# Preparing the first expert block inside the last attention unit, in a fused cross-attention and mixture-of-experts kernel

## What is computed

```python
x = x + tanh(g_xattn) * attention(k=ctx, v=ctx, q=layernorm(x))    # 16 heads of 16, relative bias, causal
x = x + tanh(g_ffn)   * moe(layernorm(x))

# moe, for N = 4096 rows, 8 experts (H = 256, I = 128) and one shared expert:
scores = sigmoid(x @ gate_w.T)                      # choose 2 of 4 groups, then 4 of 8 experts
cw     = 2.5 * normalised scores of the chosen experts, 0 for the others
out    = sum_e cw[:, e] * ((silu(x @ Wg[e]) * (x @ Wu[e])) @ Wd[e]) + shared(x)
```

## Time and profile before

| | us |
|---|---|
| median of 3 runs (683.05 to 684.8) | 683.97 |
| the profiled execution, its own time | 685.87 |
| its span, first to last instruction | 684.1 |
| PE busy | 593.5 (87%) |
| DVE busy | 429.0 (63%) |
| ACT busy | 293.7 (43%) |
| POOL busy | 197.0 (29%) |

### The profile page before, as it was taken

How to read it: one execution, slowest core, us unless ns; L and a number is a source line. 1 busy time by engine, 2 the same in 40 slices (tenths; PEclk the granted TensorE clock), 3 DMA queues, 4 the chain that set the end, 5 groups by cost and what they waited for, 6 DMA issues and landing times.

```text
span 684.1 us, 10534 instructions
## 1 busy us (share of the span) xinstructions
PE 593.5 (87%) x3256; PEld 462.2 (68%) x3256; DVE 429.0 (63%) x868; ACT 293.7 (43%) x553; POOL 197.0 (29%) x187
## 2 busy tenths in 40 slices
PE   3637897888888988886669999999999999999996
PEld 3526654556557656543458888788888888888886
DVE  5397759765877587712773856647476574756553
ACT  2443595447744685553513424233342422434221
POOL 4173035301640064001102233423323232332222
PEclk9877999999979999989679999999999999999999
DMA  5782527153433443632121031221202222031220
GB/s 168 174 213 74 115 54 176 25 126 67 120 85 83 99 119 76 173 124 51 33 78 47 6 104 47 93 61 49 76 30 93 61 78 77 1 108 47 93 63 31
DMA packets 43313, 58.13 MB, mean 85 GB/s; under 512 B 8368, under 2 KB 25520, under 8 KB 43248
## 3 DMA queue, kind: packets, MB, share of 16 engines
q1 hardware_dynamic: 42320, 56.16, 30.4%
q10 hardware_dynamic: 960, 1.57, 1.0%
HBM read 33.13 MB, written 6.11 MB: 57 GB/s over the span
## 4 chain that ended last, share of the span: by engine, by line
PE 42%; issue 28%; DVE 13%; POOL 9%; ACT 3%; DMA 2%; SPq 1%; ACTq 1%; DVEq 0%; POOLq 0%
PE py L1554 6%; PE pg L1539 6%; PE pu L1539 6%; POOL hl L1246 4%; PE work L1024 3%; PE oT L1009 3%; PE smax L944 3%; PE oT L1013 2%; DVE mx L675 2%; POOL d L454 2%; PE work L918 2%; PE sT L989 2%; PE sT L988 2%; DVE mx L703 2%; PE work L880 1%
## 5 line engine op out<-in xcount | busy, mean ns | idle before, releaser
L1246 POOL TENSOR_TENSOR hl<-sg,hh 128x512 fp32r<-128x512 f32 x72 | 93.1, 1294 | 244.0 <-ACT hh L1289 231.6
L575 ACT ACTIVATE ex<-sT 128x512 f32<-128x512 f32 (+1 forms) x160 | 92.5, 592 | 93.5 <-PE sT L989 72.8
L1283 ACT ACTIVATE sg<-pg 128x512 f32<-128x512 f32 x72 | 43.1, 598 | 196.1 <-PE pu L1539 196.0
L675 DVE TENSOR_REDUCE mx<-smax 128x2 f32<-128x308 f32 x187 | 81.4, 472 | 30.4 <-PE smax L944 29.3
L1554 PE MATMUL py<-wxl,hh 128*128 128x256 f32 x288 | 81.4, 283 | 4.1 <-DVE x L1433 2.9
L1554 PE MATMUL py<-wxh,hl 128*128 128x256 f32 x288 | 80.5, 280 | 0.0
L1554 PE MATMUL py<-wxh,hh 128*128 128x256 f32 x288 | 80.4, 279 | 0.0
L1421 DVE TENSOR_TENSOR sg<-cwb,sg 128x512 f32<-128x512 f32 x64 | 60.0, 937 | 11.2 <-DMA cwb<-cwt_d 8.3
L1539 PE MATMUL pg<-x2l,wxh 128*128 128x512 f32 x144 | 60.8, 422 | 4.1 <-issue 4.1
L1554 PEld LDWEIGHTS py<-wxl,hh 128*128 128x128 f32 x288 | 54.2, 188 | 10.3 <-DVE x L1433 5.2
L1416 DVE TENSOR_TENSOR sg<-pu,sg 128x512 f32<-128x512 f32 x72 | 49.1, 682 | 17.2 <-ACT sg L1283 15.5
(11 more groups left out here) (164 smaller groups left out, 1140.7 us busy)
## 6 DMA issues: line engine op xcount, KB each, us to landing
cwb<-cwt_d SPq DMA_DIRECT2D x64, 256.0 KB, 3.3
qs<-qh SPq DMA_DIRECT2D x56, 128.0 KB, 2.5
at<-rden_d SPq DMA_DIRECT2D x64, 64.0 KB, 2.2
out<-x SPq DMA_DIRECT2D x8, 512.0 KB, 4.5
ks<-km SPq DMA_DIRECT2D x16, 231.0 KB, 3.4
qs<-ql SPq DMA_DIRECT2D x28, 128.0 KB, 2.5
wx<-in_wx SPq DMA_DIRECT2D x9, 384.0 KB, 6.3
x<-in_x SPq DMA_DIRECT2D x3, 1024.0 KB, 13.6
```

The lines of the kernel that those rows point to most:

```text
L575: nc.scalar.activation(ex[:, g % 2, i % 5, q0:HALF], ST[i % 2][:, q0:HALF], ACT.Exp).then_inc(exp_s, 1)
L675: nc.vector.reduce_max(mx[:, first_tile(p) if start else m_tile(h, p), stk::NSTK], banks[q % len(banks)][:, 0:PAIR].rearrange("p (j k) -> ...
L1246: nc.gpsimd.tensor_tensor(hl[:, i % R, :], sg[:, i % R, :], hh[:, i % R, :], ALU.subtract).then_inc(hl_done, 1)
L1283: nc.scalar.activation(sg[:, i % R, :], PG[i % RG][:], ACT.Silu).then_inc(sg_s, 1)
```

## The change

Parts of the preparation of block 0 are moved into the last attention unit, and the order of the transition is written anew.

- **Memory.** The attention tiles `d0, d1, relc, rotc, relr, tp, sx, km` are allocated earlier, so that what the experts' stage writes early lies over tiles that are no longer used once unit 6's scores are made (`near_done`). `wxh` and `wxl` become halves of one tile `split`.
- **The last divisors.** For unit 7 the broadcast reciprocals and the divided result lie in `ex[:, 0, 0:2, :]` in place of `at` (`outputs`). `raw_done` is gone from PE.
- **Inside unit 7**, by step `i`, each engine calls `prepare`. DVE: step 0 statistics, router tables, split of expert 0 (both parts now by DVE); 4 `normalised(0)`; 7 and 10 `x_lo`; 11 split of expert 1; 13 `router_out`; 15 `logits_in` and split of expert 2; 19 `divide` of unit 6. PE: 7 and 10 `transposes`, 13 `router`, 15 `logits`. ACT: 7 and 10 `x_hi`, 19 `scores(0)`. POOL: `rstd_of(0)` and the clearing of `gst`.
- **Behind unit 7**, PE: `gate_up` 0 and 1, `weights_T`, `project(B-1, 0)`, `gate_up` 2, `project(B-1, 1)`, `gate_up` 3, then the items with those four left out. ACT: high parts of experts 3 to 8 with silu 0 and 1 among them. DVE: the order below.

```diff
+    def near_done(eng):
+
+        eng.wait_ge(st_ps, NI * (2 * B - 1))
...
+    def outputs(u):
+
+        return ex[:, 0, 0:2, :] if isinstance(u, int) and u == 2 * B - 1 else at
...
+        def prepare():                      # POOL
+            near_done(pool)
+            nc.gpsimd.memset(gst[:].bitcast(F32), 0.0).then_inc(gst_s, 1)
+            pool.wait_ge(c_in, 3 * 16)
+            rstd_of(0)
...
+        def prepare(i):                     # ACT
+            if i == 0:
+                near_done(act)
+            if i in (7, 10):
+                x_hi(0, 0, ((i - 7) // 3,))
+            if i == 19:
+                scores(0)
+
+        attend_scalar(act, prepare)
+        scores_done(act)
+        for e in range(NOWN, NE1):
             act.wait_ge(w_in[e], 16)
             nc.scalar.copy(wxh[:, e, :], wx[:, e, :]).then_inc(w_hi, 1)
-            if e == 4:
-                scores(0)
-        silu(0, 0)
+            if e in (4, 6):
+                silu(0, (e - 4) // 2)
...
+        def weights_split(e):               # DVE
+
+            dve.wait_ge(w_in[e], 16)
+            nc.vector.tensor_copy(wxh[:, e, :], wx[:, e, :]).then_inc(w_own, 1)
+            dve.wait_ge(w_own, e + 1)
+            nc.vector.tensor_tensor(wxl[:, e, :], wx[:, e, :], wxh[:, e, :], ALU.subtract).then_inc(w_lo, 1)
...
+            if i == 0:
+                near_done(dve)
+                dve.sem_inc(misc_free, 1)
+                norm_stats(0)
+                tables()
+                weights_split(0)
+            if i == 4:
+                normalised(0)
+            if i in (7, 10):
+                x_lo(0, 0, ((i - 7) // 3,))
+            if i == 11:
+                weights_split(1)
+            if i == 13:
+                router_out(0)
+            if i == 15:
+                logits_in(0)
+                weights_split(2)
+            if i == 19:
+                divide_first()
+
+        reciprocals_second, residual_first, divide_second, residual_second = attend_vector(dve, prepare)
+        scores_done(dve)
+        dve.sem_inc(gu_free, RG)
+        dve.sem_inc(h_done, R)
+        routing(0, 0)
+        routing(0, 1)
+        weights_lo(3)
+        reciprocals_second()
+        weights_in(0)
+        gated(0, 0)
+        weights_lo(4)
         residual_first()
+        gated(0, 1)
         norm_stats(1)
-        for e in range(NE1):
...
+        divide_second()
+        for e in range(5, NE1):
+            weights_lo(e)
+        weighted(0, 0)
+        weighted(0, 1)
+        residual_second()
         turns(dve, item)
...
+        def prepare(i):                     # PE
+            if i == 7:
+                pe.wait_ge(c_in, 3 * 16)
+                transposes(0, (0,))
+            if i == 10:
+                transposes(0, (1,))
+            if i == 13:
+                pe.wait_ge(gst_s, 2)
+                router(0, 0)
+            if i == 15:
+                logits(0)
+
+        attend_first, attend_finish = attend_tensor(pe, prepare)
+        exp_done(pe)
+        pe.sem_inc(hid_free, R)
+        pe.sem_inc(gu_ps, 1)
         gate_up(0, 0)
         gate_up(0, 1)
         weights_T(0)
+        attend_first()
+        gate_up(0, 2)
         attend_finish()
+        gate_up(0, 3)
         residual_done(pe)
         turns(pe, item)
```

More of the change, by code:

```diff
@@ L391, in sync, with gpsimd @@
         divisors(2 * B - 1, 1)
-    def gpsimd(pool):
+    def gpsimd(pool, prepare):
         nc.gpsimd.memset(va[:], 0.0).then_inc(pool_set, 1)
@@ L491, in unit @@
                 short_chunk(b + 1)
+            if h == 1 and not ahead:
+                prepare()
         rstd_of(0)
@@ L499, in gpsimd, with scalar @@
         batches(pool, unit)
-    def scalar(act):
+    def scalar(act, prepare):
         act.wait_ge(w_in, 5 * 16)
@@ L597, in unit @@
                     k_hi(b + 1, W[(NW0 + K_USE) % 2])
+                if h == 1 and not ahead:
+                    prepare(i)
                 if (h == 0 or ahead) and i == 19:
@@ L620, in scalar, with vector @@
         raw_out(2 * B - 1, 1, 3)
-    def vector(dve):
+    def vector(dve, prepare):
         dve.wait_ge(pool_set, 4)
@@ L808, in unit @@
                             residual(b - 1 + h, 1 - h, pr, NW0 + Y_USE[h] + pr)
+                if h == 1 and not ahead:
+                    prepare(i, lambda: divide(u - 1, 1 - h))
         dve.wait_ge(x_first, 16)
@@ L848, in first_half @@
                 residual(B - 1, 0, pr, NW0 + Y_USE[1] + pr)
-            reciprocals(2 * B - 1)
         def second_half():
@@ L854, in second_half, with tensor @@
                 residual(B - 1, 1, pr, NW0 + Y_USE[0] + pr)
-        return lambda: divide(2 * B - 2, 0), first_half, lambda: divide(2 * B - 1, 1), second_half
-    def tensor(pe):
+        return lambda: reciprocals(2 * B - 1), first_half, lambda: divide(2 * B - 1, 1), second_half
+    def tensor(pe, prepare):
         pe.wait_ge(w_in, 5 * 16)
@@ L1082, in tensor, with first @@
             values(B - 1, 1, NG - 1, short)
-        for pr in range(2):
-            project(B - 1, 0, pr, B - 1, Y_USE[1] + pr)
+        def first():
+            for pr in range(2):
+                project(B - 1, 0, pr, B - 1, Y_USE[1] + pr)
         def finish():
@@ L1142, in experts @@
     cw = sb("cw", [P, TB, E])
+    split = sb("split", [P, NE1, 2, XW], F32R)
+    wxh, wxl = split[:, :, 0, :], split[:, :, 1, :]
     cwb = sb("cwb", [P, RC, HALF])
@@ L1170, in experts @@
     block = ctx.enter_context(nc.Block())
-    RG = 2
+    RG, NOWN = 2, 3
     PER = 2 * NE1
@@ L1252, in item @@
                 rstd_of(n + 2)
-        rstd_of(0)
+        def prepare():
[3 more added lines that the diff above has]
+            rstd_of(0)
+        attend_gpsimd(pool, prepare)
+        scores_done(pool)
+        pool.sem_inc(hl_done, R)
         rstd_of(1)
@@ L1292, in item @@
             n, e, ahead = place(k, i, last)
-            if not (last and i == PER - 1):
+            if not (last and i == PER - 1) and not (isinstance(k, int) and k == 0 and i == 0):
                 silu(k, i + 1)
@@ L1409, in weights_in, with gated, weighted @@
             nc.vector.nop().then_inc(misc_free, 1)
-        def product(k, i):
+        def gated(k, i):
+            m = PER * k + i
+            dve.wait_ge(sg_s, m + 1)
+            nc.vector.tensor_tensor(sg[:, i % R, :], PU[i % RG][:], sg[:, i % R, :], ALU.mult).then_inc(gu_free, 1)
+        def weighted(k, i):
             m = PER * k + i
             u, e = divmod(i, NE1)
-            dve.wait_ge(sg_s, m + 1)
-            done = nc.vector.tensor_tensor(sg[:, i % R, :], PU[i % RG][:], sg[:, i % R, :], ALU.mult)
-            done.then_inc(gu_free, 1)
             dve.wait_ge(gu_free, m + RG + 1)
@@ L1438, in item @@
             slot = (i // NE1 + 1) % 2
-            product(k, i)
+            if not (isinstance(k, int) and k == 0 and i < 2):
+                gated(k, i)
+                weighted(k, i)
             if ahead and e == 7:
@@ new lines, in tables, with prepare @@
+        def tables():
+            dve.wait_ge(c_in, 3 * 16)
+            nc.vector.tensor_copy(gwh[:], gw[:]).then_inc(tab_s, 1)
+            dve.wait_ge(tab_s, 1)
+            nc.vector.tensor_tensor(gwl[:], gw[:], gwh[:], ALU.subtract).then_inc(tab_s, 1)
+            dve.wait_ge(tab_s, 2)
+            dve.wait_ge(gst_s, 1)
+            nc.vector.tensor_copy(gst[:, :, 0:E], gwh[:].bitcast(F32))
+            nc.vector.tensor_copy(gst[:, :, E:2 * E], gwl[:].bitcast(F32)).then_inc(gst_s, 1)
+        def prepare(i, divide_first):
+            if i == 0:
[17 more added lines that the diff above has]
+                divide_first()
@@ L1460, in _ @@
+        reciprocals_second, residual_first, divide_second, residual_second = attend_vector(dve, prepare)
[9 more added lines that the diff above has]
+        weights_lo(4)
         residual_first()
+        gated(0, 1)
         norm_stats(1)
-        for e in range(NE1):
-            dve.wait_ge(w_hi, e + 1)
-            nc.vector.tensor_tensor(wxl[:, e, :], wx[:, e, :], wxh[:, e, :], ALU.subtract).then_inc(w_lo, 1)
-            if e == 0:
-                x_lo(0, 0)
-            if e == 2:
-                router_out(0)
-            if e == 3:
-                logits_in(0)
-                routing(0, 0)
-                routing(0, 1)
-                divide_second()
-            if e == 4:
-                weights_in(0)
-            if e == 5:
-                residual_second()
+        divide_second()
@@ L1563, in item @@
             n, e, ahead = place(k, i, last)
-            if not (last and i + 2 >= PER):
+            if not (last and i + 2 >= PER) and not (isinstance(k, int) and k == 0 and i < 2):
                 gate_up(k, i + 2)
@@ L1574, in item @@
                 weights_T(n + 1)
-        transposes(0)
-        router(0, 0)
-        logits(0)
-        raw_done(pe)
+        def prepare(i):
[13 more added lines that the diff above has]
+        pe.sem_inc(gu_ps, 1)
         gate_up(0, 0)
```

61 lines of the change are left out of this document (15 added, 46 removed).

## The result

The changed kernel took 666.12 us (median of 4 runs, 665.19 to 667.02) against 684.23 for the kernel before beside it (4 runs): ratio 0.9726, interval 0.9693 to 0.9759. The gain of 18.1 us is larger than the forecast 14.2, and the time lies 0.4 us under the range. In two further sets of runs, on two different chips (e_changed_again, e_changed_third), the same kernel gave 669.05 against 684.93 (ratio 0.9767, 0.9736 to 0.9798) and 670.44 against 686.42 (0.9785, 0.9737 to 0.9832), gains of 15.9 and 16.0.

What follows compares the result with a forecast made beforehand. PE was taken to bound the experts' stage. Old equivalent 364.1 (361.3 + 2.8), less the new 349.6 and 0.3 for handovers, gave a gain of 14.2 us: 671.7 against the profiled 685.87, 670 against the median; range 666.5 to 677.

Steps and rivals of the forecast that it cites:

- Unit 7 grows by 3.1: Last attention unit: the inserted preparation lengthens it by 3.1 us, bounds 1.9 and 8; last value products end at 320.2.
- PE goes on at once behind unit 7: After unit 7: gate groups 0 and 1, weight transposes, first projection and gate group 2 run without waits to 332.8.
- DVE behind unit 7 is the new bound: Transition: DVE's work up to `weighted` 0 holds the second projection's release until 339.4, so PE stands 6.6 us.
- The second projection, 6.0: Transition, after PE's wait: its 16 matmuls take 6.0 us, between 3.69 at full clock and 6.66 at half.
- The rest as before, 0.3 lost: Block 1's preparation onward: PE stays full for some 320 us; handovers without a gate group between them cost 0.3 us.
- unit 7 was shorter than forecast, not longer: Rival, unit 7: waits in the engines' queues make it grow 8 us, not 3.1; time 675 or 676; chance 0.20.
- the gate groups started on time: Rival, behind unit 7: a late `gu_free` delays the first gate groups, PE stands 4 us; time 674; chance 0.08.
- the clock in unit 7 stayed at 1.00: Rival, unit 7: TensorE falls to half clock, up to 16.6 us lost; time 686, or 678 for half; chance 0.04.
- The rival of a short wait: Transition: quick copies and a full-clock projection save 2.3 us, DVE a further 1; time 666.5; chance 0.10.

Runs made afterwards that it cites:

- e_best: Changed kernel with release directly behind unit 7's division, separate weight tiles, and DVE's weighted products ahead of the low parts of experts 6 to 8: 669.35 us.
- e_dve_more: Changed kernel with two more DVE instructions between block 1's statistics and unit 7's division: PE's wait before the second projection 4.96 us.
- e_release_mid: Changed kernel with the second projection's release moved directly ahead of the two weighted products, behind the low parts: PE's wait 2.04 us, 23.79 us to the transposes.
- e_addresses: Kernel before, its instruction order kept, with every tile at its address in the changed kernel: 324.25 us from block 1's transposes to the end, one execution.
- e_layout: Kernel before with only the changed kernel's allocation order of the attention tiles: 685.3 us against 685.08, ratio 1.0007.
- e_early_release: Changed kernel with the second projection's release moved from behind the weighted products to directly behind unit 7's division: 664.9 us against 685.08 for the kernel before.
- e_both: Changed kernel with the release directly behind unit 7's division and `split` starting at a multiple of 64 bytes: 665.63 us, beside 670.44 for the changed kernel.

## Why the prediction was too small

The direction was right, the time 0.4 us outside the range. Point by point, with the first pair of profiles, whose spans differ by 18.9:

- **Unit 7 grows by 3.1**: it grew by 1.93. The step that was mis-sized is the readiness of the rows. The tables took 0.6 (not 0.9), the copy on DVE 0.58 (not 0.93), POOL was done 0.7 sooner, and its company cost nothing: it had ended at 297.2, before `xn` began, and `xn` took 1.37. The rows were ready at 299.04 and the transposes ran at 299.19 without a wait, so the exponential of step 8 was 0.5 late, not 1.4. The second copy on ACT (0.5) and the router (0.93) cost what they were put at; the logits cost nothing. The Trainium skill's rule (SBUF — State Buffer, on the port pair that VectorE and GpSimd share), by which the unit would have been longer, did not show there: the copy of 0.58 ran beside POOL's reciprocal deviation, and later copies without POOL took 0.55. The subtractions of 2.05 and 2.02 in e_best are as that rule says.
- **PE goes on at once behind unit 7**: right. Groups 0 and 1, transposes, projection and group 2 ran at full clock.
- **DVE behind unit 7 is the new bound**: this is the step that failed. The place of the wait, its releaser's line and its size (5.26, 6.6 forecast, 5 to 8 named) were near, but the last link was another. I let the release come with DVE's work on `weighted` 0, 4.4 us after the division, as the queue "runs one instruction ahead". The row at 346.97 does not show that: there the last wait ahead of the release was for the copy of the routing weights, done at 346.6, and what stood behind it went by at once. The release came 3.3 after it, set by the landing of the second `cwb` broadcast, while DVE's engine was still on the subtractions. e_dve_more and e_release_mid show it. The broadcasts of `cwb` are no term of the sum at all; that the size came near is luck, since 5.26 is set by when they land. With the division 0.5 earlier than forecast, PE started 1.7 us sooner, counted from the last values.
- **The second projection, 6.0**: 5.99, and 5.20 and 5.13 in the repeats.
- **The rest as before, 0.3 lost**: 1.1 lost in this pair (321.06 against 322.78 less the 2.8 of gate group 3), and even that is flattering. In the kernel before PE stood 1.16 us at 442.97, a stand that the traces show in some executions of either kernel; this one of the changed kernel has none, so its loss is really some 2.0. About 1.5 of it is the addresses, which the sum had at nothing: e_addresses, with one such stand as well, has 324.25 against 322.78. The other 0.5 lies between the transposes of blocks 1 and 2 (39.09, where 41.13 less the gate group's 2.8, with 0.2 for the addresses, would give 38.5); that is what the forecast 0.3 stood for.
- **The start**: 2.5 us of the 18.9 lie ahead of everything that changed. e_layout and the repeats show them as scatter, and they are why the first pair of runs looks better than the later two.

Without the 2.5 the pair gives 16.4, near the 15.9 and 16.0 of the repeats. Against the forecast's 14.2 the known terms are 1.2 (unit 7) and 1.8 (transition), less 0.8 (rest): 2.2. The others of the 3.9 us between 14.2 and 18.1 are this scatter. The repeats' times, 669.05 and 670.44, lie beside the forecast 670, but that is partly luck: they come from a unit 7 and a transition put 3 to 4 us too long and a rest put up to 1.7 too short.

Of the rivals none came: unit 7 was shorter than forecast, not longer, the gate groups started on time, and the clock in unit 7 stayed at 1.00. The rival of a short wait named 666.5 and had the direction of the miss, but its reason was the copies and a projection at full clock; only the copies were quicker.

## What to carry to other kernels

Work that is a chain of handovers is cheap between the steps of a loop whose engines have holes and dear behind it: the same instructions cost 1.9 and 8.0 us here. A release that one engine gives to another belongs directly behind what it depends on: it passes with the queue, not with the engine, so computing instructions ahead of it cost little (up to six here) and an unmet wait ahead of it can cost all of that wait. For the same reason it must not stand for the end of work: that has to come from the working instruction's own semaphore. When a gain of a few us is judged against a program whose start and clock scatter by as much, compare stretches inside the executions, not ends alone.

## What the runs showed of the hardware

- DVE's queue passed six instructions that its engine hadn't finished, 4.8 us of work, up to a semaphore increment behind them (e_release_mid).
- Moving tiles to other addresses, with no change of instructions, made 12 matmuls of 256 columns 0.02 to 0.04 us slower, a block of 41.1 us 0.15 to 0.4 us longer and the expert stage some 1.5 us (e_addresses). Neither interleaving nor a start at a multiple of 64 bytes mattered.
- A copy of 128 x 768 float32 to fp32r on DVE, both in SBUF, takes 0.55 to 0.58 us, the subtraction of the same size 0.96.
- The point at which TensorE's clock comes back after a wait differs between executions: the same 16 matmuls after the same wait of 2.31 us took 5.23 or 6.66, which moves all that follows by 1.4 us. After a wait of 2.0 to 2.2 us the clock fell in one profile (e_release_mid) and stayed in three (e_early_release, e_both, e_best).
- A subtraction on DVE with both inputs in SBUF and a subtraction on POOL at the same time took 2.0 us each, against 0.95 and 1.3 alone (e_best).
